# A fifth border in the tile order of an attention and mixture-of-experts block, with the last batch finished in two halves

## What is computed

```python
x = L0_attn_embeddings
x = _layernorm(x + _L0_attn_ref(x, W_Q, W_K, W_V), axis=-1)
x = _layernorm(x + _L0_ffn_ref(x, gate_w, gate_b, w1, b1, w2, b2, ln_g, ln_b), axis=-1)
...
# inside _L0_ffn_ref
topk_vals, topk_idx = jax.lax.top_k(logits, TOP_K)          # TOP_K = 2, 8 experts
h = jax.nn.gelu(jnp.einsum('bsd,edf->bsef', x, w1) + b1, approximate=False)
expert_out = jnp.einsum('bsef,efd->bsed', h, w2) + b2       # d = 128, f = 512
out = jnp.einsum('bse,bsed->bsd', gate_probs, expert_out)
out = (out - mu) / jnp.sqrt(var + EPS) * ln_g + ln_b
```

## Time and profile before

| | before |
|---|---|
| runs, median | 265.51 us (262.98, 265.51, 265.73) |
| the profiled execution, its own time | 265.34 us |
| its span from first to last instruction | 263.6 us |
| PE busy | 231.7 us (88%) |
| PEld busy | 211.9 us (80%) |
| DVE busy | 171.6 us (65%) |
| ACT busy | 178.7 us (68%) |
| POOL busy | 143.5 us (54%) |

### The profile page before, as it was taken

How to read it: one execution, slowest core, us unless ns; L and a number is a source line. 1 busy time by engine, 2 the same in 40 slices (tenths; PEclk the granted TensorE clock), 3 DMA queues, 4 the chain that set the end, 5 groups by cost and what they waited for, 6 DMA issues and landing times.

```text
span 263.6 us, 7258 instructions
## 1 busy us (share of the span) xinstructions
PE 231.7 (88%) x1867; PEld 211.9 (80%) x1868; DVE 171.6 (65%) x952; ACT 178.7 (68%) x524; POOL 143.5 (54%) x165
## 2 busy tenths in 40 slices
PE   1799899899999899999999999999999999998000
PEld 1457687787887799999999999999999999998000
DVE  0043768688888878557943333366488999899854
ACT  2256675787784879988875565565556996699921
POOL 8300004727777677777877777756544446456400
PEclk9999999999999979999999999999999999999655
DMA  4999210221221345442527798758789586814192
GB/s 128 247 330 328 50 42 23 90 61 54 90 92 61 79 133 134 126 114 83 123 63 194 249 328 239 250 166 240 230 283 352 152 232 189 281 34 121 49 309 81
DMA packets 44801, 42.38 MB, mean 161 GB/s; under 512 B 5440, under 2 KB 33520, under 8 KB 44768
## 3 DMA queue, kind: packets, MB, share of 16 engines
q1 hardware_dynamic: 40448, 33.10, 44.1%
q0 software_dynamic: 4320, 8.92, 9.7%
HBM read 27.89 MB, written 12.01 MB: 151 GB/s over the span
## 4 chain that ended last, share of the span: by engine, by line
PE 59%; DVE 15%; DMA 8%; ACT 5%; DVEq 4%; issue 4%; SPq 3%; POOL 1%; POOLq 0%; ACTq 0%
PE bank L561 16%; PE bank L572 15%; PE bank L422 6%; PE bank L449 6%; DMA pair<-returned 5%; PE bank L408 3%; DVEq L1169 2%; PE bank L489 2%; PE bank L470 2%; DVE sum_stats L1108 2%; PE bank L437 2%; DMA returned<-x,slot_back 2%; PE bank L413 2%; ACT probs L653 2%; DVE pair L1135 2%
## 5 line engine op out<-in xcount | busy, mean ns | idle before, releaser
L725 ACT ACTIVATE h<-bank,b_cols 128x128 f32<-128x128 f32 x284 | 81.6, 382 | 37.7 <-PE bank L561 37.3
L1303 POOL DMA_INDIRECT slots<-rows,slot_of x64 | 64.3, 1004 | 58.1 <-DVE rows L954 39.8
L1308 POOL DMA_INDIRECT returned<-x,slot_back x71 | 71.1, 1002 | 44.9 <-DVE x L1089 35.7
L572 PE MATMUL bank<-w_all,h 128*128 x568 | 78.6, 282 | 0.0
L561 PE MATMUL bank<-slot_xT,w_now 128*128 128x128 f32 x568 | 75.0, 275 | 0.0
L572 PEld LDWEIGHTS bank<-w_all,h 128*128 128x128 f32 x568 | 69.0, 192 | 0.8
L561 PEld LDWEIGHTS bank<-slot_xT,w_now 128*128 128x128 f32 x568 | 69.1, 192 | 0.1
L854 DVE CAST slot_back<-slot_x 128x1 uint32<-128x1 f32 x71 | 10.4, 146 | 40.0 <-PE bank L561 40.0
L811 DVE TENSOR_REDUCE negmax<-bank 128x1 f32<-128x128 f32 (+3 forms) x32 | 14.7, 485 | 21.2 <-PE bank L423 21.0
L449 PEld LDWEIGHTS bank<-v,probsT 128*128 128x128 f32 x160 | 20.4, 198 | 5.7 <-issue 3.8
L1089 DVE TENSOR_SCALAR x<-bank,slot_gate 128x128 f32<-128x128 f32 x71 | 23.9, 340 | 0.0
(11 more groups left out here) (151 smaller groups left out, 302.2 us busy)
## 6 DMA issues: line engine op xcount, KB each, us to landing
w_now<-in_L_ffn_w_dram SPq DMA_DIRECT2D x47, 256.0 KB, 3.3
slot_x<-slots SPq DMA_DIRECT2D x71, 65.0 KB, 2.9
w_all<-in_L_ffn_w_dram SPq DMA_DIRECT2D x16, 256.0 KB, 5.5
pair<-returned SPq DMA_DIRECT2D x16, 256.0 KB, 3.1
x<-n_L_attn_embeddings_dram SPq DMA_DIRECT2D x8, 256.0 KB, 4.5
rows<-rows SPq DMA_DIRECT2D x8, 256.0 KB, 2.8
returned<-x,slot_back POOLq DMA_INDIRECT x71, 3.4
slots<-rows,slot_of POOLq DMA_INDIRECT x64, 2.3
```

Of the source, the lines that this page charges most:

```text
L572: m = nc.tensor.matmul(o, h[:, s % RING, c * P:(c + 1) * P], w2_c, start=False, stop=(c == FC - 1))
L725: m = nc.scalar.activation(h[:, s % RING, cols], bank_[:, cols], ACT.Gelu, bias=b1_cols[:, c:][:, bass.ds(first, 1)])
L1303: g_.indirect_dma_start(slots, bass.IndirectOffsetOnAxis(ap=slot_of[:, b, c:c + 1], axis=0), rows[:, k, b * TB + t, :], None).then_inc(dis ...
L1308: g_.indirect_dma_start(returned, bass.IndirectOffsetOnAxis(ap=slot_back[:, j:j + 1], axis=0), y[:, j % Y_RING, :], None).then_inc(y_retur ...
```

## The change

A fifth border is put between the borders 63 and 71, at 67: all tiles that hold rows of the first seven and a half batches come before tile 67. The borders are now counted in half batches. The last batch becomes two groups of two tiles (28, 29 and 30, 31): each is loaded, added, normalised and stored by itself. The number of tiles, 71, stays.

```diff
-    PARTS = (4, 6, 7, 8)
+    HALF = TB // 2
+    PARTS = (4 * 2, 6 * 2, 7 * 2, 7 * 2 + 1, 8 * 2)
...
-    WHOLE = [b * TB * TOPK + E - 1 for b in PARTS]
+    WHOLE = [b * HALF * TOPK + E - 1 for b in PARTS]
...
-        LAST_ACT = TB // 2
...
-        ROOTS = ((0, 4), (0, 6), (4, 6), (6, 7), (6, 7), (7, 8), (7, 8))
+        LAST_ACT = HALF // 2
+        LAST_TILES = NT - HALF
+        ROOTS = ((0, 4 * TB), (0, 6 * TB), (4 * TB, 6 * TB), (6 * TB, 7 * TB), (6 * TB, 7 * TB),
+                 (7 * TB, LAST_TILES), (7 * TB, LAST_TILES), (LAST_TILES, NT), (LAST_TILES, NT))
...
+        def tiles_of(b):
+
+            return range(LAST_TILES, NT) if b == B else range(b * TB, LAST_TILES if b == B - 1 else (b + 1) * TB)
...
             load_pair(B - 2)
             wait_whole(3)
             load_pair(B - 1)
+            wait_whole(4)
+            load_pair(B)
...
-            for b, parts in ((4, 1), (5, 1), (6, 1), (7, 2)):
+            for b, parts in ((4, 1), (5, 1), (6, 1), (7, 1), (8, 2)):
...
-            normalise_late(7, 6, late_ready[7], LAST_ACT)
+            take_root(7)
+            normalise_late(7, 6, late_ready[7])
+            take_root(8)
+            normalise_late(8, 8, late_ready[8], LAST_ACT)
...
-                    if b + 1 in PARTS:
-                        k = PARTS.index(b + 1)
+                    if 2 * b + 1 in PARTS:
+                        k = PARTS.index(2 * b + 1)
+                        vec.tensor_copy(totals[:, k * E:(k + 1) * E], place[0:1, HALF * E:(HALF + 1) * E])
+                    if 2 * b + 2 in PARTS:
+                        k = PARTS.index(2 * b + 2)
                         vec.tensor_copy(totals[:, k * E:(k + 1) * E], running[0:1, 1 - buf, :])
...
-                add_pair(7)
-                take_moments(7)
-                finish_root(4)
-                centre_times_g(7)
-                finish_root(5)
-                dve.drain()
-                times_rstd_plus_x(7)
-                take_moments(7)
-                finish_root(6)
+                for b in (7, 8):
+                    add_pair(b)
+                    take_moments(b)
+                    finish_root(2 * b - 10)
+                    centre_times_g(b)
+                    finish_root(2 * b - 9)
+                    dve.drain()
+                    times_rstd_plus_x(b)
+                    take_moments(b)
+                finish_root(8)
                 dve.drain()
-                for t in range(7 * TB + LAST_ACT, 8 * TB):
+                for t in tiles_of(8)[LAST_ACT:]:
```

More of the change, by code:

```diff
@@ L223, in moe_block @@
         y_returned = [sem(f"y_returned{s}") for s in range(Y_RING)]
-        pair_loaded = [sem(f"pair_loaded{b}") for b in range(B)]
+        pair_loaded = [sem(f"pair_loaded{b}") for b in range(B + 1)]
         normed, res_ready = sem("normed"), sem("res_ready")
         aggregated, rooted, scaled = sem("aggregated"), sem("rooted"), sem("scaled")
-        late_ready = {b: sem(f"late_ready{b}") for b in (4, 5, 6, 7)}
+        late_ready = {b: sem(f"late_ready{b}") for b in (4, 5, 6, 7, 8)}
         stored = sem("stored")
@@ L246, in moe_block @@
         NORM_FROM, NORM_AT, OUT_AT, ROOT_AT = 2 * TB, 55, 67, (52, 65)
-        LAST_ACT = TB // 2
-        ROOTS = ((0, 4), (0, 6), (4, 6), (6, 7), (6, 7), (7, 8), (7, 8))
+        LAST_ACT = HALF // 2
+        LAST_TILES = NT - HALF
+        ROOTS = ((0, 4 * TB), (0, 6 * TB), (4 * TB, 6 * TB), (6 * TB, 7 * TB), (6 * TB, 7 * TB),
+                 (7 * TB, LAST_TILES), (7 * TB, LAST_TILES), (LAST_TILES, NT), (LAST_TILES, NT))
         def root_tiles(r):
-            return slice(ROOTS[r][0] * TB, ROOTS[r][1] * TB)
+            return slice(*ROOTS[r])
+        def tiles_of(b):
+            return range(LAST_TILES, NT) if b == B else range(b * TB, LAST_TILES if b == B - 1 else (b + 1) * TB)
         @block.sync
@@ L298, in load_pair @@
             def load_pair(b):
+                tiles, batch = tiles_of(b), min(b, B - 1)
                 for k in range(TOPK):
-                    sp.dma_start(pair[:, k, b * TB:(b + 1) * TB, :],
-                                 returned[k * N + b * S:k * N + (b + 1) * S, :].rearrange("(p t) d -> p t d", p=P)).then_inc(pair_loaded[b], 16)
+                    back = returned[k * N + batch * S:k * N + (batch + 1) * S, :].rearrange("(p t) d -> p t d", p=P)
+                    sp.dma_start(pair[:, k, tiles.start:tiles.stop, :],
+                                 back[:, tiles.start - batch * TB:tiles.stop - batch * TB, :]).then_inc(pair_loaded[b], 16)
             def wait_whole(n):
@@ L390, in _ @@
             sp.dma_start(out_p[:, 0:EARLY, :], pair[:, 1, 0:EARLY, :]).then_inc(stored, 16)
-            for b, parts in ((4, 1), (5, 1), (6, 1), (7, 2)):
+            for b, parts in ((4, 1), (5, 1), (6, 1), (7, 1), (8, 2)):
+                tiles = slice(tiles_of(b).start, tiles_of(b).stop)
                 sp.wait_ge(late_ready[b], parts)
-                sp.dma_start(out_p[:, b * TB:(b + 1) * TB, :], pair[:, 1, b * TB:(b + 1) * TB, :]).then_inc(stored, 16)
-            sp.wait_ge(stored, 16 * 5)
+                sp.dma_start(out_p[:, tiles, :], pair[:, 1, tiles, :]).then_inc(stored, 16)
+            sp.wait_ge(stored, 16 * 6)
         @block.tensor
@@ L747, in normalise_late @@
                 act.wait_ge(scaled, r + 1)
-                for k in range(b * TB, b * TB + n):
+                for k in tiles_of(b)[0:n]:
                     m = scale_and_shift(k)
@@ L1101, in add_pair @@
             def add_pair(b):
-                tiles = slice(b * TB, (b + 1) * TB)
+                tiles = slice(tiles_of(b).start, tiles_of(b).stop)
                 dve.wait_ge(pair_loaded[b], 16 * TOPK)
@@ L1106, in take_stats @@
             def take_stats(b):
-                for t in range(b * TB, (b + 1) * TB):
+                for t in tiles_of(b):
                     vec.bn_stats(sum_stats[:, t, :], pair[:, 0, t, :])
             def aggregate(b):
-                for t in range(b * TB, (b + 1) * TB):
+                for t in tiles_of(b):
                     m = vec.bn_aggr(sum_moments[:, t, :], sum_stats[:, t, :])
```

2 lines of the change are left out of this document (1 added, 1 removed).

## The result

| | before | after |
|---|---|---|
| median of 20 runs | 263.56 us | 261.26 us |
| lowest, highest | 262.76, 266.02 | 259.89, 263.29 |
| ratio, 95% interval | | 0.9915 [0.9893, 0.9936] |
| the profiled execution, its own time | 265.34 us | 262.94 us |
| its span | 263.6 us | 261.1 us |

The change saves 2.3 us, where 1.2 were forecast, and the time lies under the stated range. Part of the distance is the starting point: with more runs, before has 263.56 and not the 265.51 (or the profiled 265.34) that the sum was made from. The other part, 1.1 us, is in the sum itself.

What follows compares the result with a forecast made beforehand. TensorE was taken to bound the kernel to about 189 us, then returns and loads of `pair`, with the DVE at the end. End -2.1 and table +0.9 gave -1.2 from 265.34: 264.1 us, range 262.5 to 266.2.

Steps and rivals of the forecast that it cites:

- The end: Last batch in two halves: DVE ends 1.2 us earlier, last scaling saves 0.4, last store 0.5; sum -2.1 us.
- rival 4: End of the kernel: halves keep most of their time, 4.6 us each, the second ending at 259.1; 265.3 us, chance 0.10.
- case 2: Table costs nothing, 263.2 us; lower end, with the DVE's groups halving exactly, put at 262.8; chance 0.26.
- The table: Near 125 to 138 us: table ready 1.15 us later, delaying tile 24's load and TensorE; net +0.9 us.
- rival 2: Table costs nothing because tile 24's load, issued 1.15 later, lands in 2.9 us or less; 263.2 us, chance 0.26.
- the step 21 that isn't late: Sign at TensorE near 138 us: if step 21 isn't late, the forecast is wrong and the table costs nothing.
- rivals 3 and 5: TensorE's wait for tile 24 lowers its clock: 3 gives 265.2 us, chance 0.12; 5, twice as long, 266.3, chance 0.10.
- rival 3: TensorE's wait near 138 us brings its clock down, costing 1.07 us; 265.2 us, chance 0.12.

Runs made afterwards that it cites:

- the table alone: The kernel before with only the fifth border in the table, the last batch still loaded after tile 71 and finished in one piece; ratio 1.0009.
- before with the early table: The kernel before, with four borders, and the table's pieces one DVE step (2 us) earlier; ratio 0.9967.
- both halves at 71: The changed kernel with both halves of the last batch loaded after tile 71; ratio 0.9983.
- three and one, early table: The changed kernel with the last border at 69 (three tiles, then one) and the table one DVE step earlier; ratio 0.9914.
- early table: The changed kernel with the table's pieces one DVE step (2 us) earlier, first set; ratio 0.9887.
- early table, tile 11 first: The changed kernel with the table one DVE step earlier and slot tile 11 loaded ahead of the 256 KB copy of rows; ratio 0.9944.
- early table, again: The changed kernel with the table one DVE step earlier, measured once more in a second set; ratio 0.9880.
- three and one: The changed kernel with the last border at 69, so three tiles and then one; ratio 0.9899, median 260.86 us.
- changed, second profile: The changed kernel itself, unaltered, measured again beside other variants on one chip; ratio 0.9937, 261.41 us.
- changed, tile 11 first: The changed kernel with the load of slot tile 11 issued ahead of the 256 KB copy of rows; ratio 0.9943.
- six borders: The changed kernel with one more border in the table alone, used by nothing, to make the table another 1.15 us late; ratio 0.9978.
- seven borders: The changed kernel with two more borders in the table alone, used by nothing, to make the table 2.3 us later; ratio 1.0036.

## Why the prediction was right or wrong

**The end: right, a little small.** The block of two was put at 4.0 us and took 3.92, so rival 4 is out. The store was to land in 1.8 us and did. (The 0.3 that the prediction worked out by the Trainium skill for the halved store was too little: 0.5 went. The section "Anatomy of one DMA" of "DMA: Bandwidth & Descriptors" gives its fit for DMAs that GpSimd issues, and this one is issued by SP.) The first half's loads were in at 246.0, 3.6 us before the DVE came for them (2.6 forecast), and the experiment that took this cover away got its wait back. The DVE ended 1.55 us earlier (1.2 forecast): 0.16 of the difference is the two blocks of 3.92 instead of 4.0, and 0.18 that batch 6 ended earlier (249.74, not 249.92). The last scaling gave 0.4 and the store 0.5, as forecast. From the last `expand` to the end of the span it is 25.8 us in before and 23.3 in after: 2.5 less. The other profiles agree: 25.4 with the table alone, 25.8 in before with the early table and 25.3 with both halves at 71; 23.2 to 23.9 in eight other profiles with the first part of the batch early (the execution of 266.9 us left out). Between the mean of the three profiles that load the whole batch late and of the nine that load the first part early it is 2.3, the whole measured gain of 2.3. (The stated bound of -2.5 for the end is a slip: with the groups halving exactly the terms give -2.6, and case 2 has its lower end at 262.7.)

**The table: the delay right, its price wrong.** The step that failed is "Moved by 1.15, the load lands at 139.4 and TensorE waits 1.3 us instead of 0.18". It took the landing of 3.8 us from the one profiled execution as the load's own length ("There is no cover left at all") and carried it along. What the runs showed, in all 14 profiles, by how far ahead of TensorE the load of tile 24 was issued (all in us):

| kernel | issued ahead | 15 of 16 parts in | last part in | `instruction` packet | TensorE waits for it | over 2.0 a step, at tiles 24 and 25 |
|---|---|---|---|---|---|---|
| before, early table | 4.9 | 2.0 | 3.2 | 0.7 to 2.1 | no | 0 |
| three and one, early table | 3.8 | 1.8 | 2.5 | 2.1 to 3.0 | no | 0.53 |
| early table | 3.8 | 1.9 | 2.3 | 1.9 to 2.9 | no | 0.54 |
| early table, tile 11 first | 3.8 | 1.8 | 3.6 | 1.2 to 2.5 | no | 0.33 |
| early table, again | 3.7 | 1.8 | 3.0 | 0.9 to 1.9 | no | 0 |
| before | 3.6 | 2.1 | 3.8 | 1.0 to 2.7 | 0.18 | 0.57 |
| before's end, five borders | 2.5 | 1.9 | 2.8 | -0.1 to 1.3 | 0.32 | 0.48 |
| three and one | 2.5 | 1.8 | 2.8 | 0.5 to 1.4 | 0.33 | 0.50 |
| halves at 71 | 2.5 | 2.0 | 2.9 | -0.1 to 1.5 | 0.49 | 0.65 |
| changed, second profile | 2.5 | 1.8 | 2.8 | -0.3 to 1.3 | 0.35 | 0.58 |
| changed, first profile | 2.4 | 1.9 | 1.9 | -1.8 to -0.5 | no | 0 |
| changed, tile 11 first | 2.4 | 1.8 | 1.9 | -1.4 to -0.4 | no | 0 |
| six borders | 1.05 | 1.9 | 1.9 | -0.9 to 0.5 | 0.91 | 1.07 |
| seven borders | 0.6 | 2.1 | 2.1 | -1.0 to 0.2 | 1.55 | 1.8 |

"Issued ahead" is from SP's issue to the moment at which TensorE's weight load of the slot tile was free to start (its start less its wait). The next three columns count from SP's issue too. A load is moved in 16 parts, and each reports in the trace when it is done; the "landed after" of the experiments above ends at TensorE's start and is at most 0.06 more than the last part's time. The `instruction` packet is one of 16 KB that another DMA queue moves near this place in every execution. Its rows in the DMA views of before and after, each of a stretch of 0.1 us (from 135.4 and from 134.4), give packets, MB, and the packet's time as a share of the 16 engines' 0.1 us, so 1.69 and 1.34 us:

```profile
q8 instruction: 1, 0.02, 105.4%
...
q8 instruction: 1, 0.02, 83.8%
```

All parts of the load but one are thus in after 1.8 to 2.1 us in every execution. In the four executions in which the packet was over no later than 0.5 us behind the issue, all 16 parts came together. In the other ten a single part came 0.5 to 1.7 us behind the other 15, and by least (0.5 and 0.6) in the two in which the packet began only when the 15 were in. So the 3.8 of before is a load of 2.1 us with one part that came 1.7 late, and behind the other 15 parts there were 1.6 us of cover, of which the change took 1.2. Tile 11 in the changed kernel's first profile is the same: issued at 108.27, 15 parts in after 2.1 us, the last after 4.1, with such a packet from 110.14 to 111.17. That the packet holds the part back fits all 14 profiles; but no experiment moved the packet, and the trace doesn't say which of the 16 engines carried it, so the mechanism is likely and not shown. What sets the packet's moment against the load's, which shifts by 3.9 us among the profiles, stays open.

The first 1.2 us of delay (3.6 to 2.4 ahead) left the last column at 0 to 0.65, where before had 0.57 already, and the next 1.4 (to a lead of 1.05) cost some 0.4 to 1.1 more. So the term was 0 and not +0.9 (in the pair of profiles of before and after -0.57), inside the 0 to +0.9 that the text gave it; -2.1 with nothing lost is rival 2, which had 0.26 of the chances and gave 263.2, 0.8% under its own base against 0.85% measured. The prediction named what would decide (the step 21 that isn't late), but chose the end of the bound that came from a single record, the extreme one of 71. Of the 1.1 us by which the sum is off, this term is 0.9 and the end 0.2.

**The clock: rivals 3 and 5 did not happen.** TensorE waited for tile 24 in seven profiles, 0.18 to 1.55 us, and behind none of these waits did its clock fall. But a wait for tile 11 was followed by one: in the execution of 266.9 us, with three tiles and one, TensorE waited 1.18 us for that tile, and from 114.7 to 118.1 its clock was 1.2 GHz (weight load; then the stretch of 4 us with the engines' busy time and the granted clock).

```profile
113.77 0.14 PEld L501 LDWEIGHTS bank<-ident,slot_x 128*128 128x128 f32 x1 [1.18 <-DMA slot_x<-slots]
...
114.00:118.00 4.00, 4.00 (x23) 3.92 (x23) 1.27 (x9) 0.78 (x4) 3.09 (x4) 0.59 0.42 115
```

The wait of 1.19 us for the same tile in the changed kernel's first profile was followed by no fall. So the runs put rival 3 out for tile 24 and don't put it out in general.

**The base.** The profiled execution of before carries the dip near 93 us, which the prediction priced at 1.07 us. Its page in the kernel before with the early table has none:

```profile
PEclk9999999999999999999999999999999999999655
```

So executions of nearly the same program differ in whether they have it. But it is not what makes before's record long. From the wait for `xnT` at 88 to 90 us to the `expand` of step 10 it is 27.6 us in before and 27.4 with the early table. Over the profiles it is 27.3 to 27.7 with this dip and 27.3 to 27.5 without it, less the waits for slot tiles (the execution of 266.9 us left out). What before's execution lost lies ahead: up to its wait for `v`, the same program needed 27.81 us there and 25.90 in the kernel with the early table. 0.8 of these 1.9 us are there at matmuls of line 408 already (8.20 and 7.42), and the rest is the pace of the matmuls behind them (timeline of PE, before and the early table):

```profile
15.89 1.72 PE L422 MATMUL bank<-xT,gT 128*128 128x512 f32 x2
...
14.62 1.08 PE L422 MATMUL bank<-xT,gT 128*128 128x512 f32 x2
```

The clock row has a 9 there in both and doesn't show this difference. In all 14 profiles that wait for `v` lies between 25.7 and 27.8 us, and before's is the latest. Of the three runs that the forecast had, two lay at 265.5 or above, where the median over 20 is 263.56. The range was laid around 265.34 and 265.51, 1.8 to 1.95 us above what before has over 20 runs. Without that the forecast's -1.2 would have stood at 262.4, within 0.5% of the measured time.

## What to carry to other kernels

When the last wait of a kernel is for data that come in one piece, look for an earlier point at which part of it is whole. The gain is the work that fits into the wait, not the split as such: split without the earlier border, the same work saved 0.2%, not to be told from nothing. Before a term is carried from one place to another, ask whether its duration is its own. A DMA's time to landing from one record can hold something else's time: here one part of 16 came 1.7 us behind the rest, beside a packet of another queue that did not move with the load. The median of its kind, with the extreme as a bound, was the better value. And where the base is three runs that spread by 1%, the range must carry the base's own uncertainty, not the change's alone.

## What the runs showed of the hardware

- A load of 65 KB has 15 of its 16 parts in 1.8 to 2.1 us after its issue, at one place of the program in 14 executions. The last part comes up to 1.7 us later, where a 16 KB packet of the `instruction` queue, 1.0 to 1.7 us long, is under way more than 0.5 us behind the issue. That the packet is the cause is likely from the times, and not shown.
- The dip of TensorE's clock to 1.2 GHz, 3.4 us long, comes and goes between executions of nearly the same program, and has had three places. It lay near 93 us in before, after, and the experiments with the table alone, with tile 11 first and with the early table (both times); near 51 us in the kernel with tile 11 first and the early table, in that with seven borders and in that with three tiles and one, which had a second one from 114.7 us; and nowhere in five other profiles. One of those near 51 us, as a stretch of 4 us (busy time of the engines, then the granted clock):

```profile
50.00:54.00 4.00, 4.00 (x23) 3.00 (x22) 1.80 (x12) 1.50 (x5) 0.96 (x1) 0.66 0.10 33
```

- Waits of TensorE stand ahead of these places, and don't decide it. In the profile with the dip near 51 us, the timeline of PE has this wait for `xnT` 2 us ahead of it:

```profile
47.07 1.06 PE L482 MATMUL bank<-gw,xnT 128*128 128x8 f32 x8 [0.95 <-ACT xnT L647]
```

- All 14 profiles have this wait of 0.95 us near 47 us and again near 89 us. The changed kernel's second profile has the second one here, and its clock falls at neither place:

```profile
87.95 1.06 PE L482 MATMUL bank<-gw,xnT 128*128 128x8 f32 x8 [0.95 <-ACT xnT L647]
```

- So the same wait is followed by a fall in one execution and not in another, and the longer single wait of 1.55 us at 141 was followed by none. What makes the difference isn't shown.
- What a dip costs depends on its place. Between the two waits for `xnT` it is 42.9 to 43.0 us in the three profiles with the dip near 51 us and 41.3 in the others: 1.6 us. The dip near 93 us, in which the prediction saw 1.07 us of slower matmuls, leaves no loss by step 10.
